# A slot map built from two bf16 maps, eight one-hot columns at a time, in place of one float32 map

## The reference

```python
scores = jax.nn.softmax(xt @ wg, axis=-1)
gates_k, idx_k = jax.lax.top_k(scores, K)              # K = 2 of E = 8 experts
masks = jax.nn.one_hot(idx_k, E, dtype=jnp.int32)
m = jnp.transpose(masks, (1, 0, 2)).reshape(K * T, E)
loc = jnp.sum((jnp.cumsum(m, axis=0) - 1) * m, axis=-1) # place among the rows of its expert
valid = (loc < cap)                                     # cap = 2 T / E = 4096
disp = zeros((E, cap, D)).at[idx_k, loc].add(x * valid) # row -> slot
out = relu(disp @ w1 + b1) @ w2 + b2                    # per expert
y = sum_k gates_k * valid * out[idx_k, loc]
```

## Time and profile before

| | |
|---|---|
| median of three runs | 4012.66 us (4011.36 to 4013.64) |
| profiled execution | 4012.38 us, of which the trace's span is 4010.7 us |
| busy in the span | TensorE 3328.8 us, VectorE 3699.5, ScalarE 2529.3, GpSimd 3252.5 |
| stage 3 in the trace | first one-hot at 200.92 us, first load of the main loop at 342.62 us |
| granted TensorE clock, mean | 0.958 of 2.4 GHz |

### The profile page before, as it was taken

The page is one execution under the profiler, slowest core; times in us unless marked ns, Lnnn a source line. Parts: engine busy times, 40 slices in busy tenths (PEclk is TensorE's granted clock), DMA queues, the critical chain, the costliest instruction groups (busy, mean ns, idle before and its releaser), DMA issues.

```text
span 4010.7 us, 70861 instructions
## 1 busy us (share of the span) xinstructions
PE 3328.8 (83%) x16548; PEld 2166.8 (54%) x16548; DVE 3699.5 (92%) x2500; ACT 2529.3 (63%) x4779; POOL 3252.5 (81%) x1722
## 2 busy tenths in 40 slices
PE   7697788888887888888887888878887888888887
PEld 4375555555555555555555555555555555555554
DVE  6797999989999999999998999989999999999997
ACT  3213666766666667666666667667666667666665
POOL 0004989888888989888898999889888999888886
PEclk9898999999999999999999999999999999999998
DMA  9954666565666656575666656575667656575666
GB/s 326 342 75 117 158 152 154 137 164 150 161 151 171 156 147 146 138 177 151 157 159 167 159 146 148 138 173 157 160 154 172 156 142 148 138 178 149 158 160 155
DMA packets 382792, 646.23 MB, mean 161 GB/s; under 512 B 86717, under 2 KB 258881, under 8 KB 382081
## 3 DMA queue, kind: packets, MB, share of 16 engines
q1 hardware_dynamic: 289458, 539.05, 48.6%
q0 software_dynamic: 67776, 85.24, 13.8%
q10 hardware_dynamic: 25104, 16.91, 1.9%
HBM read 515.68 MB, written 142.80 MB: 164 GB/s over the span
## 4 chain that ended last, share of the span: by engine, by line
issue 27%; POOL 26%; PE 12%; SPq 11%; DVE 8%; DMA 7%; ACT 6%; POOLq 1%; ACTq 1%; DVEq 0%
POOL u L1003 16%; SPq L331 7%; PE bank L627 5%; POOL out_rows L962 5%; DMA dt<-dt_rows 3%; DVE h L1194 3%; PE bank L574 3%; POOL xg L950 3%; DVE hc L1183 3%; SPq L319 3%; ACT bank L775 2%; DMA dt<-x 2%; DMA w_sb<-w 2%; ACT ht L817 1%; PE bank L534 1%
## 5 line engine op out<-in xcount | busy, mean ns | idle before, releaser
L1003 POOL TENSOR_TENSOR u<-dtx,b_sb 128x1024 f32<-128x1024 f32 x1024 | 2492.4, 2494 | 232.9 <-DVE h L1194 203.8
L1194 DVE TENSOR_TENSOR_SCAN h<-bank,u 128x1024 f32<-128x1024 f32 x1024 | 2302.3, 2277 | 44.0 <-ACT bank L775 30.6
L775 ACT ACTIVATE bank<-dt,a_neg 128x1024 f32<-128x1024 f32 x1026 | 1129.0, 1108 | 548.7 <-DMA dt<-dt_rows 247.3
L627 PE MATMUL bank<-xgt,w_sb 128*128 128x256 f32 x4096 | 1088.2, 412 | 349.9 <-ACT ht L817 163.6
L1183 DVE TENSOR_TENSOR hc<-h,bank 128x2048 f32<-128x2048 f32 x514 | 1165.0, 2267 | 175.8 <-ACT bank L845 175.2
L627 PEld LDWEIGHTS bank<-xgt,w_sb 128*128 128x128 f32 x4096 | 782.1, 201 | 746.4 <-issue 650.7
L636 PE MATMUL bank<-w_sb,ht 128*128 128x256 f32 x4096 | 938.8, 382 | 49.5 <-ACT o_sb L832 32.3
L636 PEld LDWEIGHTS bank<-w_sb,ht 128*128 128x128 f32 x4096 | 762.4, 190 | 244.6 <-issue 149.2
L817 ACT ACTIVATE ht<-bank,b_sb 128x256 f32<-128x256 f32 x1024 | 424.0, 464 | 313.6 <-PE bank L627 279.4
L586 PE MATMUL bank<-hc,rsum 128*32 128x512 f32 x4112 | 552.7, 610 | 4.2 <-DVE hc L1183 4.2
L962 POOL DMA_INDIRECT out_rows<-o_sb,sidx x258 | 415.6, 1611 | 124.8 <-issue 65.0
(11 more groups left out here) (105 smaller groups left out, 1866.9 us busy)
## 6 DMA issues: line engine op xcount, KB each, us to landing
b_sb<-bc_rows SPq DMA_DIRECT2D x1032, 128.0 KB
c_sb<-bc_rows SPq DMA_DIRECT2D x1032, 128.0 KB
dt<-dt_rows SPq DMA_DIRECT2D x528, 128.0 KB, 4.4
dtx<-dtx_rows SPq DMA_DIRECT2D x528, 128.0 KB, 2.8
w_sb<-w SPq DMA_DIRECT2D x18, 1024.0 KB, 9.8
dt_rows<-dt_n SPq DMA_DIRECT2D x137, 128.0 KB, 3.1
dtx_rows<-dtx_n SPq DMA_DIRECT2D x137, 128.0 KB
out_rows<-y_sb POOLq DMA_DIRECT2D x34, 512.0 KB
```

Of the source, the lines that this page charges most:

```text
L627: mm = pe.matmul(m_ps[:, c, :], w1_sb[:, kk, ch * P:(ch + 1) * P], xgt[:, kk, :], start=(kk == 0), stop=(kk == KD - 1))
L775: act.activation(a_ps[k % 2], dt[:, k % GPP, :], ACT.Exp, scale=a_neg[:, col:col + 1]).then_inc(a_ready, 1)
L1003: pool.tensor_tensor(u[:, k % UB, :], dtx[:, gp, :], b_sb[:, j, :], ALU.mult).then_inc(u_ready, 1)
L1194: dve.tensor_tensor_scan(h[:, k, :], a_ps[k % 2], u[:, k % UB, :], 0.0, ALU.mult, ALU.add).then_inc(scan_done, 1)
```

## The change

The map becomes two maps in the halves of one PSUM bank. `map_low` sums the partition of the choice plus one, `map_high` its column number. Both have values exact in bf16, and L1166 puts them together as 128 * high - 1, then plus low. All one-hots are bf16, written for eight columns by one instruction each, with the eight columns as four pairs: the two columns of a pair lie side by side in memory. `oh_p` and `oh_c` are plain one-hots. `oh_high` is `oh_p` times the column number (VectorE), `oh_low` is `oh_p` times the partition number plus one (a new ScalarE instruction, `low_part`). TensorE does two bf16 matmuls for each column. The buffers hold two blocks of eight. New copies make the bf16 constants and the bf16 `prt` and `col`. The core of the diff:

```diff
-        tokval = sb("tokval", [P, 2 * NT])
+        tokval = sb("tokval", [P, 1])
+        iota_pair = sb("iota_pair", [P, E * LPE, 2], BF16)
+        col_h = sb("col_h", [P, 2 * NT], BF16)
+        prt_h = sb("prt_h", [P, 2 * NT], BF16)
+        num_h = sb("num_h", [P, 2 * NT], BF16)
...
+        oh_c = hc[:, 4:8].bitcast(BF16).rearrange("p a t -> p (a t)").rearrange("p (s i c r) -> p s i c r", s=2, c=E * LPE, r=2)
+        oh_p, oh_low, oh_high = (u[:, i, :].bitcast(BF16).rearrange("p (s i c r) -> p s i c r", s=2, c=P, r=2)
+                                 for i in range(1, 4))
...
+        OHP = OHB // 2
 # TensorE
             with pe.Fori(0, NG) as q:
                 prep(q, 0, q)
-                with pe.Fori(0, OHQ) as o:
+                for o in range(OHQ):
+                    n = q * OHQ + o
+                    pe.wait_ge(oh_ready, n + 1)
+                    pe.wait_ge(low_ready, n + 1)
                     for r in range(OHB):
-                        n = (q * OHQ + o) * OHB + r
-                        pe.wait_ge(oh_ready, n + 1)
-                        pe.matmul(map_ps, oh_p[:, r, :], oh_c[:, r, :], start=False, stop=True,
-                                  skip_group_check=True).then_inc(oh_used, 1)
+                        i, k = r // 2, r % 2
+                        pe.matmul(map_low, oh_low[:, o % 2, i, :, k], oh_c[:, o % 2, i, :, k],
+                                  start=False, stop=True, skip_group_check=True)
+                        mm = pe.matmul(map_high, oh_high[:, o % 2, i, :, k], oh_c[:, o % 2, i, :, k],
+                                       start=False, stop=True, skip_group_check=True)
+                    mm.then_inc(oh_used, 1)
 # ScalarE
+            def low_part(n, buf):
+                act.wait_ge(ohp_done, n + 1)
+                act.activation(oh_low[:, buf].rearrange("p i c r -> p (i c r)"),
+                               oh_p[:, buf].rearrange("p i c r -> p (i c r)"), ACT.Copy,
+                               scale=tokval[:, 0:1]).then_inc(low_ready, 1)
+
             with act.Fori(0, NG) as q:
-                evac_prep(q)
-                act.wait_ge(v_done, q + 1)
-                softplus(q)
-                log_part(q)
+                for o in range(OHQ):
+                    low_part(q * OHQ + o, o % 2)
+                    if o == 0:
+                        evac_prep(q)
+                        act.wait_ge(v_done, q + 1)
+                    if o == 1:
+                        softplus(q)
+                    if o == 2:
+                        log_part(q)
 # VectorE
+            dve.tensor_copy(num_h[:], iota[:])
+            dve.tensor_copy(iota_pair[:], iota[:].unsqueeze(2).to_broadcast([P, E * LPE, 2]))
...
-            dve.sem_inc(oh_used, OHB)
+            link(dve.tensor_copy(prt_h[:], prt_f))
+            link(dve.tensor_copy(col_h[:], col_f))
+            dve.sem_inc(oh_used, 2)
...
+            def pairs(t, g, n):
+                return t[:, bass.ds(g * OHB, OHB)].rearrange("p (i r) -> p i r", r=2).unsqueeze(2).to_broadcast([P, OHP, n, 2])
             with dve.Fori(0, NG) as q:
-                with dve.Fori(0, OHQ) as o:
-                    for r in range(OHB):
-                        i = (q * OHQ + o) * OHB + r
-                        if r % (OHB // 2) == 0:
-                            dve.wait_ge(oh_used, i + OHB // 2)
-                            dve.tensor_tensor(oh_p[:, r:r + OHB // 2, :],
-                                              iota[:, 0:P].unsqueeze(1).to_broadcast([P, OHB // 2, P]),
-                                              prt_f[:, bass.ds(i, OHB // 2)].unsqueeze(2)
-                                              .to_broadcast([P, OHB // 2, P]), ALU.is_equal)
-                        dve.tensor_scalar(oh_c[:, r, :], iota[:], col_f[:, bass.ds(i, 1)],
-                                          tokval[:, bass.ds(i, 1)], ALU.is_equal, ALU.mult).then_inc(oh_ready, 1)
+                for o in range(OHQ):
+                    g, buf = q * OHQ + o, o % 2
+                    dve.wait_ge(oh_used, g + 1)
+                    settle(dve)
+                    dve.tensor_tensor(oh_p[:, buf], wide(iota_pair, P), pairs(prt_h, g, P), ALU.is_equal).then_inc(ohp_done, 1)
+                    dve.tensor_tensor(oh_c[:, buf], wide(iota_pair, E * LPE), pairs(col_h, g, E * LPE), ALU.is_equal)
+                    dve.wait_ge(ohp_done, g + 1)
+                    dve.tensor_tensor(oh_high[:, buf], oh_p[:, buf], pairs(num_h, g, P), ALU.mult).then_inc(oh_ready, 1)
                 prep_dt(q)
...
-            link(dve.tensor_scalar(map_f[:], map_ps, -1.0, None, ALU.add))
+            link(dve.tensor_scalar(map_f[:], map_high, float(P), -1.0, ALU.mult, ALU.add))
+            link(dve.tensor_tensor(map_f[:], map_f[:], map_low, ALU.add))
```

More of the change, by code:

```diff
@@ L121, in ssm_moe @@
         tmp_i, tmp_i2 = (hc[:, 3, n * NT:(n + 1) * NT].bitcast(I32) for n in range(2))
-        oh_c = hc[:, 4:8].rearrange("p a t -> p (a t)").rearrange("p (r c) -> p r c", r=8)
+        OHB = 8
+        oh_c = hc[:, 4:8].bitcast(BF16).rearrange("p a t -> p (a t)").rearrange("p (s i c r) -> p s i c r", s=2, c=E * LPE, r=2)
         gates = sb("gates", [P, NT, 2])
@@ L126, in ssm_moe @@
         lt_sb = u[0:E, 0, :].rearrange("p (a t) -> p a t", a=2)
-        OHB = 8
-        oh_p = u[:].rearrange("p a t -> p (a t)")[:, 0:OHB * P].rearrange("p (r c) -> p r c", r=OHB)
+        oh_p, oh_low, oh_high = (u[:, i, :].bitcast(BF16).rearrange("p (s i c r) -> p s i c r", s=2, c=P, r=2)
+                                 for i in range(1, 4))
         map_f = sb("map_f", [P, E * LPE])
@@ L160, in ssm_moe @@
         m_ps = bank[:, 7, :].rearrange("p (c s) -> p c s", s=SL)
-        map_ps = bank[:, 4, 0:E * LPE]
+        map_ps = bank[:, 4, :]
+        map_low, map_high = map_ps[:, 0:E * LPE], map_ps[:, E * LPE:2 * E * LPE]
         z_ps = bank[:, 6, 0:KD * Q]
@@ L193, in ssm_moe @@
         oh_used = sem("oh_used")
+        ohp_done = sem("ohp_done")
+        low_ready = sem("low_ready")
         map_cleared = sem("map_cleared")
@@ L1145, in _, with wide @@
             col_f = col.rearrange("p k i -> p (k i)")
-            dve.sem_inc(oh_used, OHB)
-            with dve.Fori(0, NG) as q:
-                with dve.Fori(0, OHQ) as o:
-                    for r in range(OHB):
-                        i = (q * OHQ + o) * OHB + r
-                        if r % (OHB // 2) == 0:
-                            dve.wait_ge(oh_used, i + OHB // 2)
-                            dve.tensor_tensor(oh_p[:, r:r + OHB // 2, :],
-                                              iota[:, 0:P].unsqueeze(1).to_broadcast([P, OHB // 2, P]),
-                                              prt_f[:, bass.ds(i, OHB // 2)].unsqueeze(2)
-                                              .to_broadcast([P, OHB // 2, P]), ALU.is_equal)
-                        dve.tensor_scalar(oh_c[:, r, :], iota[:], col_f[:, bass.ds(i, 1)],
-                                          tokval[:, bass.ds(i, 1)], ALU.is_equal, ALU.mult).then_inc(oh_ready, 1)
+            link(dve.tensor_copy(prt_h[:], prt_f))
+            link(dve.tensor_copy(col_h[:], col_f))
+            dve.sem_inc(oh_used, 2)
+            def wide(t, n):
+                return t[:, 0:n, :].unsqueeze(1).to_broadcast([P, OHP, n, 2])
+            def pairs(t, g, n):
+                return t[:, bass.ds(g * OHB, OHB)].rearrange("p (i r) -> p i r", r=2).unsqueeze(2).to_broadcast([P, OHP, n, 2])
+            with dve.Fori(0, NG) as q:
+                for o in range(OHQ):
[6 more added lines that the diff above has]
+                    dve.tensor_tensor(oh_high[:, buf], oh_p[:, buf], pairs(num_h, g, P), ALU.mult).then_inc(oh_ready, 1)
                 prep_dt(q)
@@ L1162, in _ @@
             prep_dt(NG + 1)
-            dve.wait_ge(oh_used, 2 * NT + OHB)
+            dve.wait_ge(oh_used, 2 * NT // OHB + 2)
             dst, tok = slot_dst[:, SJ:SJ + E * LPE], slot_tok[:, SJ:SJ + E * LPE]
-            link(dve.tensor_scalar(map_f[:], map_ps, -1.0, None, ALU.add))
+            link(dve.tensor_scalar(map_f[:], map_high, float(P), -1.0, ALU.mult, ALU.add))
+            link(dve.tensor_tensor(map_f[:], map_f[:], map_low, ALU.add))
             link(dve.tensor_copy(tok, map_f[:]))
@@ L1234 @@
         "iota_d": np.tile(np.arange(E * lpe, dtype=np.float32), (P, 1)),
-        "tokval_d": (1 + np.arange(2 * T // P, dtype=np.float32)[None, :] * P
-                     + np.arange(P, dtype=np.float32)[:, None]),
+        "tokval_d": 1 + np.arange(P, dtype=np.float32)[:, None],
         "rsum_d": np.tile(np.eye(P // r, dtype=np.float32), (r, 1)),
```

## The result

The changed kernel takes 3980.36 us, median of 4 runs (3972.99 to 3986.36), beside 4013.15 for the kernel before on the same chip; the ratio is 0.9916, interval 0.9894 to 0.9938. Faster, by some 33 us where 40.8 were forecast: the median lies 3.4 us above the forecast's own range (3964 to 3977) and within the range of 8 in 10 (3963 to 4001). The profiled execution is the fastest of the four, 3972.99 us with a span of 3971.3, against 3971.6 forecast. The stage alone moved by -37.5 us: the main loop's first load is at 305.12 instead of 342.62 us. From that load to the end of the span it is 3666.2 us instead of 3668.1.

A forecast was written before the change was run, and what follows sets the result against it. TensorE and VectorE were both taken as full in the slot map. Rounds of 10.25 us end TensorE's last block at 290.8 instead of 331.98 (-41.2), plus 0.45 behind it: -40.8 from 4012.38, so 3971.6 us, range 3964 to 3977.

The forecast's parts named there:

- Direction and mechanism: Slot map stage: TensorE and VectorE are both full, so relieving both makes the kernel faster, by 40.8 us in all.
- VectorE's rate: Three paired bf16 one-hot instructions per block: 0.52 ns an element, 2.36 us a block.
- rivals that priced a lesser rate: VectorE's bf16 one-hots: one element a cycle, 4031.8 us, chance 0.09; or 0.78 ns an element, 3998 us, chance 0.09.
- TensorE: Map matmuls: a bf16 load and matmul pair takes 0.115 us, a block 1.84 us, a round 8.9 us.
- the load is hidden: TensorE's bf16 pairs; the rival said the weight load isn't hidden: 0.17 us a pair, 3986.7 us, chance 0.10.
- The clock: TensorE's clock at 1.00 from 215 us on; the rival had it fall to half, 4029 us, chance 0.04.
- ScalarE: Four low_part instructions a round at 1.11 us each, 6.7 us a round in all, hidden under VectorE's 9.8.
- The touching place: Once a round VectorE waits some 0.4 us for a buffer TensorE holds through prep; the round becomes 10.25 us.
- Round 2: ScalarE waits for the bcv store, low_part ends at 223.1; VectorE finishes at 227.7 instead of 224.2, 3.5 us lost.
- Rounds 3 to 8: 6 x 10.25: The last six map rounds take 10.25 us each, 61.5 us in all, to 289.2.
- late stores: Sign of a wrong prediction: the stores of a round land later than the next round needs them.
- The tail: Chain behind the last round: same instructions at the same low clock, plus 0.45 us for one new TENSOR_TENSOR from PSUM.

## Why the prediction was right, and where it was off

*Direction and mechanism: right, and shown.* Two engines were full, both were relieved, and neither half gives anything alone (4028.15 and 4015.65). The gain was put too high: the ratio is 0.9916 and 0.9917 in the two sets of runs, where 3971.6 of 4012.38 is 0.9898.

*VectorE's rate: right.* 0.52 ns an element, block 2.34 against 2.36. The rivals that priced a lesser rate didn't occur: an input that repeats one 4-byte pair 256 times ran at the full rate. By the Trainium skill, Vector Engine (DVE) Microarchitecture Reference, section 5.2, a stream keeps its full rate only in runs of at least two adjacent 4-byte words; read as a rule on re-reads too, it is refuted by these 1.22 us.

*TensorE: right.* 0.113 us a pair against 0.115; the rows with 128 and 8 columns gave it, and the load is hidden. *The clock: right in the later rounds*, 1.00 at 90% busy, but not in round 2, as said below.

*ScalarE: right.* 1.147 us against 1.11, hidden.

*The touching place: right mechanism, small size.* 0.67 us of waiting, not 0.4, and the round 10.45, not 10.25. But the step lacked GpSimd: with the wait taken away the shared interface costs 0.54 in its place, so the round would have been 10.4 without the touching place too.

*Round 2: the wait right, its price too low*, 14.7 us against 13.8. The wait ended 0.8 us earlier than forecast, and still VectorE lost 4.2 us instead of 3.5: TensorE had stood 3.40 us, its granted clock was at the lower level behind that, and the block that VectorE waited for took 3.2 us, not the 1.84 of the full clock.

*Round 3: the step that failed.* "Rounds 3 to 8: 6 x 10.25" took the stores of a round as hidden. In 16 us a round a late store was: the kernel before had one of `dt_n` that landed after 9.3 us, and nothing waited for it. In 10 us, with 11.57 to land, it isn't. Round 3 took 12.2 us and round 4 10.6. Of round 3's excess over 10.45, 0.89 us are the wait for that store; most of the rest is the `oh_c` stretched by GpSimd (0.54), which here comes on top of a buffer wait of 0.65 in the same round. The prediction named late stores as what would make it wrong, and didn't price them.

*The tail: the +0.45 is there*, but the clock was at full speed in it for these eight pairs of `prep` (1.16 us, 1.92 in the earlier trace rows), and it took 10.27 us instead of 10.64 + 0.45. That was luck of this execution: the unaltered kernel had 1.98 us for them in its second profile, and four of its variants had 2.08, all behind the same or a longer idle time of TensorE.

The sum against the forecast of 301.9: start +0.25, round 1 -0.4, round 2 +0.9, round 3 +1.95, round 4 +0.4, rounds 5 to 8 +0.8, the last block +0.2, tail -0.8. That is +3.3, and 305.12 was measured. The main loop gave 1.9 back in the profiled run, which leaves +1.4 (3972.99 against 3971.6). That it came so near is in part chance, by the tail's clock and the 1.9: the medians, 3980.36 and 3976.91, lie 5 to 9 us above.

*What stays open:* why the main loop takes between 3662 and 3680 us in kernels that don't change it, and when the clock is at which level in the tail. The kernel before spreads from 3998.65 to 4028.78 us over all its runs as well.

## What to carry to other kernels

Where two engines are full together, price and relieve both; take one back at a time to see which half carried the gain. When a round gets shorter by a third, recheck what it used to hide: a small store behind bulk copies, a buffer's release, an instruction of an off-path engine that shares an interface with the one that leads, a pause of TensorE with the lower clock behind it. Removing one such wait often hands its time to the next, so take the shorter round's whole list before moving any of them.

## What the runs showed of the hardware

- GpSimd's TENSOR_TENSOR of 256 elements, 0.75 us alone, took 4.85 us and up to 15.93 us while VectorE issued two-input instructions without a pause. Where it took 0.77 us instead, it stretched VectorE's 1.22 us instruction to 1.77.
- One float32 input is enough to take pairing from a bf16 TENSOR_TENSOR (2.28 us against 1.22 for 2048 elements); re-reading one pair isn't.
- A TENSOR_SCALAR from float32 to bf16 with one operand per partition has 0.264 us between starts for 256 elements; the one of the kernel before with two such operands, float32 out, had 0.32.
- LDWEIGHTS and MATMUL of 256 bf16 columns, both operands read with a step of two elements: 0.113 us a pair at the full clock, 0.213 at the half.
- After TensorE had stood 3.40 us its next block ran at the half clock for some twelve of 16 pairs, 3.2 us in all.
- A bf16 ACTIVATE of 1024 elements took 1147 ns, float32 1108.
- A `dt_n` store landed after 11.57 us in the stretch in which 8-byte packets of another store were under way; moving those away removed the wait for it.
